# Another order for one quad's second norm and its widening in a fused mixer kernel

## What is computed

```python
x = x + attn_a(layernorm(x))   # state-space mixer: 8 heads, head size 64, state 128, rotated B and C,
                               # h = alpha*h + beta*Bx_prev + gamma*Bx; y = h.C; rmsnorm; out projection
x = x + ffn(layernorm(x))      # r = sigmoid(xr @ W_r); out = r * (relu(xk @ W_k)**2 @ W_v)
x = x + attn_b(layernorm(x))   # in projection to 768 channels, causal filter of 3 taps, product of two thirds,
                               # convolution over 2048 tokens, gate by the last third, out projection
x = x + ffn(layernorm(x))      # the same ffn
```

## Time and profile before

| | us |
|---|---|
| median of the 3 runs | 4767.65 (4763.98 to 4768.28) |
| profiled execution | 4775.44 |
| its span | 4773.7 |

### The profile page before, as it was taken

How to read it: one execution, slowest core, us unless ns; L and a number is a source line. 1 busy time by engine, 2 the same in 40 slices (tenths; PEclk the granted TensorE clock), 3 DMA queues, 4 the chain that set the end, 5 groups by cost and what they waited for, 6 DMA issues and landing times. The chain is left out here.

```text
span 4773.7 us, 118783 instructions
## 1 busy us (share of the span) xinstructions
PE 4307.8 (90%) x39924; PEld 3574.9 (75%) x39924; DVE 3254.1 (68%) x6762; ACT 2160.8 (45%) x5049; POOL 2349.4 (49%) x3277
## 2 busy tenths in 40 slices
PE   5259999999999999999999999999978999989999
PEld 4128777777777777777777777777756888878888
DVE  8456666667676666666676666666644666658888
ACT  3124444444444444444444444444435666645555
POOL 3027666566655666566566656665520000006666
PEclk9669999999999999999999999999988999999999
DMA  8120111111111111111111111111007666643333
GB/s 271 78 79 27 33 47 37 38 41 37 47 37 33 46 37 45 37 35 45 37 41 40 37 45 35 35 47 37 30 29 193 181 185 179 181 124 101 105 104 97
DMA packets 369422, 347.40 MB, mean 73 GB/s; under 512 B 24665, under 2 KB 342937, under 8 KB 359833
## 3 DMA queue, kind: packets, MB, share of 16 engines
q1 hardware_dynamic: 352028, 323.88, 22.8%
q10 hardware_dynamic: 16896, 16.78, 1.0%
HBM read 231.91 MB, written 108.66 MB: 71 GB/s over the span
## 5 line engine op out<-in xcount | busy, mean ns | idle before, releaser
L733 PE MATMUL bank<-w_bc,xnT 128*128 128x512 f32 x3072 | 815.8, 408 | 40.2 <-POOL xnT L1054 40.2
L733 PEld LDWEIGHTS bank<-w_bc,xnT 128*128 128x128 f32 x3072 | 570.2, 192 | 180.3 <-issue 65.6
L936 ACT COPY turned_t<-bank 128x512 f32<-128x512 f32 x512 | 299.6, 585 | 860.8 <-PE bank L756 860.7
L1467 PE MATMUL p_yc<-sig,toep 64*64 64x256 f32 (+14 forms) x16384 | 539.5, 282 | 17.1 <-issue 13.9
L1062 POOL TENSOR_TENSOR steps<-upto,par 128x512 fp32r<-128x512 f32 x512 | 550.4, 1095 | 5.6 <-PE bank L742 5.6
L1467 PEld LDWEIGHTS p_yc<-sig,toep 64*64 64x64 f32 x16384 | 476.9, 132 | 92.7 <-issue 46.3
L1171 DVE TENSOR_TENSOR rot<-bank,par 128x512 f32<-128x512 f32 x512 | 350.6, 685 | 240.8 <-PE bank L733 162.5
L1071 POOL TENSOR_TENSOR turned_b<-rot 128x512 f32<-128x512 f32 x256 | 325.1, 1270 | 308.7 <-DVE rot L1172 308.3
L766 PEld LDWEIGHTS bank<-turned_t 128*128 128x128 f32 x2048 | 301.3, 214 | 127.6 <-issue 104.9
L766 PE MATMUL bank<-turned_t 128*128 128x128 f32 x2048 | 310.5, 301 | 93.5 <-issue 92.0
L1191 DVE TENSOR_TENSOR mix<-bank,decay 128x512 f32<-128x512 f32 x256 | 175.9, 687 | 300.4 <-PE bank L766 299.9
(11 more groups left out here) (259 smaller groups left out, 9741.2 us busy)
## 6 DMA issues: line engine op xcount, KB each, us to landing
toep<-taps_dram SPq DMA_DIRECT2D x256, 260.0 KB, 4.2
el<-el_dram SPq DMA_DIRECT2D x256, 128.0 KB, 3.0
xg<-arg_x SPq DMA_DIRECT2D x32, 512.0 KB, 5.0
xnT_dram<-xt_g ACTq DMA_DIRECT2D x32, 512.0 KB, 5.1
xnT_raw<-xnT_dram SPq DMA_DIRECT2D x128, 128.0 KB, 2.3
x_quad<-arg_x SPq DMA_DIRECT2D x32, 512.0 KB, 3.9
x_dram<-x_quad SPq DMA_DIRECT2D x32, 512.0 KB, 3.7
x0T_dram<-conv SPq DMA_DIRECT2D x32, 512.0 KB, 2.8
```

Source lines behind the costliest of these rows:

```text
L733: last = mm(p_bc[c][:, :], xnT[w.q % 2][p][:, k, :], w_bc[q][:, k, c * 1024 + g * W4:c * 1024 + (g + 1) * W4], start=(n == 0), stop=(n == ...
L936: s_.copy(turned_t[g][c][:, :], p_tr[:, :]).then_inc(s[f"copy_{BC[c]}"], 1)
L1467: last = mm(by_seq(p_y[p][c][odd * H:(odd + 1) * H, 0:2 * TILES])[:, :, first:], toep[n % SLOTS][c * H:(c + 1) * H, lag * H:(lag + 1) * H] ...
```

## The change

It moves steps within the lists of PE, ACT, POOL and DVE. No instruction is added or removed.

- PE: `widen` 5 goes from behind the two first `project_bc` of q=2 to the end of q=1.
- DVE: in q=0, `residual2` 0 goes from ahead of `weigh_gram` 0 to behind `weigh_gram` 1, and `residual2` 1 from there to behind `rotate` (1,0). In q=1, both `x2_lo` go ahead of `cut_decay` 1. In q=2, `taps` 4 goes ahead of `rotate` (0,0) and `taps` 5 ahead of `weigh_gram` 0.
- POOL, q=0: `layer_rstd` 0 goes from behind `fade_state` to behind `add_turned` (1,1), `layer_rstd` 1 from behind `masked_steps` 1 to behind `add_turned` (1,0). `before_filter` stays.
- ACT: in q=0, `normalised` 0 goes behind `exponentials` 0 and `own_bounds` 1, `normalised` 1 behind `copy_turned` (0,0). In q=1 both `x2_hi` go ahead of `square_y`. In q=2 `take_up` 5 goes ahead of `own_bounds` 0.

```diff
--- before.py
+++ after.py
@@ -857,8 +857,6 @@
                 for q in range(QUAD):
                     tile(q, 0, project_bc, 0, 1)
                     tile(q, 0, project_bc, 0, 0)
-                    if q == 2:
-                        quad(2, widen, 5)
                     if q == 3:
                         quad(1, receptance, 0)
                     tile(q, 1, gram, 0)
@@ -901,6 +899,8 @@
                     if q == 2:
                         quad(1, key, 1)
                     tile(q, 0, decay_logs, 1)
+                    if q == 1:
+                        quad(2, widen, 5)
             rounds(body)
 
         @block.scalar
@@ -997,20 +997,18 @@
                 for q in range(QUAD):
                     tile(q, -1, split_xnT)
                     tile(q, 1, exponentials, 1)
-                    tile(q, 2, square_y)
-                    tile(q, 0, own_bounds, 0)
                     if q == 1:
                         quad(2, x2_hi, 0)
                         quad(2, x2_hi, 1)
+                    tile(q, 2, square_y)
                     if q == 2:
                         quad(2, take_up, 5)
+                    tile(q, 0, own_bounds, 0)
                     if q == 3:
                         quad(1, tanh, 0)
                     tile(q, 1, copy_turned, 1, 1)
                     tile(q, 1, copy_turned, 1, 0)
                     tile(q, 2, mean_square, q)
-                    if q == 0:
-                        quad(2, normalised, 2, 0)
                     if q == 1:
                         quad(2, take_up, 0)
                     if q == 2:
@@ -1021,7 +1019,7 @@
                     tile(q, 0, exponentials, 0)
                     tile(q, 0, own_bounds, 1)
                     if q == 0:
-                        quad(2, normalised, 2, 1)
+                        quad(2, normalised, 2, 0)
                     if q == 1:
                         quad(2, take_up, 1)
                         quad(2, take_up, 2)
@@ -1031,6 +1029,8 @@
                     if q == 2:
                         quad(1, relu_squared, 0)
                     tile(q, 0, copy_turned, 0, 0)
+                    if q == 0:
+                        quad(2, normalised, 2, 1)
                     if q == 1:
                         quad(1, normalised, 1, 0)
                         quad(1, normalised, 1, 1)
@@ -1141,14 +1141,15 @@
                     tile(q, 0, add_turned, 0, 0)
                     tile(q, 1, fade_state)
                     if q == 0:
-                        quad(2, layer_rstd, 2, 0)
                         quad(2, before_filter)
                     tile(q, 2, scan_rstd)
                     tile(q, 0, add_turned, 1, 1)
+                    if q == 0:
+                        quad(2, layer_rstd, 2, 0)
                     tile(q, 0, masked_steps, 1)
+                    tile(q, 0, add_turned, 1, 0)
                     if q == 0:
                         quad(2, layer_rstd, 2, 1)
-                    tile(q, 0, add_turned, 1, 0)
                     if q == 1:
                         quad(1, layer_rstd, 1, 1)
                         quad(1, first_column)
@@ -1275,22 +1276,20 @@
             def body(tile, quad, n):
                 for q in range(QUAD):
                     tile(q, 0, rotate, 0, 1)
-                    tile(q, 1, cut_decay, 1)
-                    tile(q, 0, rotate, 0, 0)
-                    if q == 0:
-                        quad(2, residual2, 0)
                     if q == 1:
                         quad(2, x2_lo, 0)
                         quad(2, x2_lo, 1)
+                    tile(q, 1, cut_decay, 1)
                     if q == 2:
                         quad(2, taps, 4)
-                    tile(q, 1, weigh_gram, 0)
+                    tile(q, 0, rotate, 0, 0)
                     if q == 2:
                         quad(2, taps, 5)
+                    tile(q, 1, weigh_gram, 0)
                     tile(q, 0, rotate, 1, 1)
                     tile(q, 1, weigh_gram, 1)
                     if q == 0:
-                        quad(2, residual2, 1)
+                        quad(2, residual2, 0)
                     if q == 1:
                         quad(2, taps, 0)
                     if q == 2:
@@ -1302,6 +1301,8 @@
                     if q == 3:
                         quad(1, gated, 0)
                     tile(q, 0, rotate, 1, 0)
+                    if q == 0:
+                        quad(2, residual2, 1)
                     if q == 1:
                         quad(2, taps, 2)
                     tile(q, 1, carry_state)
```

## The result

Over eight runs the changed kernel takes 4777.51 us (median, 4772.04 to 4783.97), and the kernel before, over eight runs, 4765.81 us (4760.48 to 4777.86). The ratio is 1.0023, with a 95% interval of 1.0012 to 1.0034: 11 us slower, 6 to 16. That is 0.37 us in each of 30 rounds. The forecast was 18 us slower, in a range from 4738 to 4815.

The account below looks back on a forecast made before the run. PE's instruction order, with its waits and low clock, was taken as the bound. Per round -0.75 (q=0), -0.8 (q=1) and +2.15 (q=2) sum to +0.6 us, +18 us over 30 rounds: 4786 us, range 4738 to 4815.

Parts of the forecast that it names:

- q=0: `x2n_over` against the old order at full clock: In q=0, `x2n_over` starts at 1097.7 instead of 1097.02: +0.7 us per round, bounds -0.4 to +1.2.
- q=0: low clock gone: In q=0, the mean clock loss behind the old wait before the second gram goes: -2.15 us per round.
- q=0: low clock behind the new waits: In q=0, two new PE stalls cost clock: 0.7 us per round, bounds 0 and 1.8.
- q=1, at full clock: In q=1, PE's gaps before `sum_over` and `widen` 0 shrink by 0.2 and 0.6 us: -0.8 us per round.
- q=2: `sum_over` later: In q=2, DVE's later chain makes `sum_over` start later: +0.95 us per round, bounds +0.8 to +1.6.
- q=2: more low clock: In q=2, clock loss grows from 0.7 to 1.9 us as PE idles nearly 3 us: +1.2 us per round.
- What goes in q=0: In q=0, PE's second gram starts without its 3.1 us wait, and the clock loss behind it leaves this place.
- What is late next: In q=0, POOL's stream delays the norm: new PE stalls of 0.7 to 1.8 us before `turn_over`, about 2 at `x2n_over`.
- rival B: Whole kernel: one of two clock terms goes the forecast's way, the other not; within 0.3 us per round, 4768; chance 0.20.
- Rival A: q=0: `x2n_over` comes at 1097.0 and its stalls don't lower the clock; -24 us, 4744; chance 0.24.
- C: q=0 and q=2: low clock at both places, and long; +3.4 us per round, 102 us; chance 0.10.
- D: Whole round: POOL and DVE keep ahead everywhere, the stalls really go; 8.3 us per round, 4519 us; chance 0.03.

Follow-up runs that it names:

- e2: Changed kernel with its q=0 part undone (second norm's residual, rstd and normalised steps as before): 4786.95 us, 1.0048 of the kernel before.
- e10: Changed kernel with `before_filter` moved behind `layer_rstd` 1 on POOL in q=0: 4765.1 us, 0.9999 of the kernel before.
- e7: Kernel before with only the q=0 part of the change added: 4737.78 us, 0.9952 of the kernel before.
- e3: Changed kernel with its q=1 part undone (`x2_hi` and `x2_lo` late again): 4789.16 us, 1.0052 of the kernel before.
- e1: Changed kernel with its q=2 part undone (`widen` 5 and its readers back in their old places): 4744.21 us, 0.9962 of the kernel before.
- e4: Changed kernel where a step taking a post bank waits only for the reader of the bank's last use: 4720.67 us, 0.9912 of the kernel before.
- e11: Changed kernel with eight extra constant-weight products on PE before `sum_over` of q=2: 4727.25 us, 0.9921 of the kernel before.
- e5: Changed kernel with `x2n_over` moved behind the first two `project_bc` of q=1: 4705.88 us, 0.9880 of the kernel before.
- e9: Changed kernel with edits of e1, e4, e5, `layer_rstd` 0 ahead of `add_turned` (1,1), q=2's `sum_over` and `xn_over` behind the second gram: 4539.16 us, 0.9533.
- e8: Kernel before with the edit of e4, one wait per use of the two post banks: 4697.00 us, 0.9861 of the kernel before.

## Why the prediction was right, point by point

All in us per round, from the changed kernel's profile, means of 29 rounds.

| step | forecast | measured |
|---|---|---|
| q=0: `x2n_over` against the old order at full clock | +0.7 | +0.7 |
| q=0: low clock gone | -2.15 | -2.15 |
| q=0: low clock behind the new waits | +0.7 | +0.3 |
| q=1, at full clock | -0.8 | -0.2 |
| q=2: `sum_over` later | +0.95 | +0.8 |
| q=2: more low clock | +1.2 | +0.8 |
| sum | +0.6 | +0.3 in the profile (100.69 against 100.46 gives 0.23), 0.37 from the runs |

*What goes in q=0* was right: no wait before L766, and e2 brings 3.1 us of it back. *What is late next* was right in its places and sizes: 1.4 us before L756, 2.2 us before L845. That POOL's stream is the reason was argued in the forecast; e10 shows it, with 1.65 us for 1.54 us of work moved.

*q=1* was mis-sized, -0.2 instead of -0.8 us. The early low parts are worth 0.6 us by themselves (`x2n_over` to `widen` 0 at full clock: 8.81 us in e7 and e3 without them, 8.18 in e1 and 8.20 in the changed kernel with them), since `widen` 0 keeps a wait of 0.25 us. And the forecast left out a loss of 0.4 us (8.44 us before, 8.81 in e7): `x2n_over`, now behind a wait, has 0.34 us of exposed waits inside that the old one, reached with a full queue, did not show. e4 shows what they are.

*q=2* was right in mechanism: the 3.1 us of idle time on DVE stood in the forecast, and so did the later `sum_over`. `sum_over` came 0.8 instead of 0.95 us later, because the cut was not held up by POOL (0.60 us in both kernels, where 0.75 was reckoned).

*The clock terms* were both too high, 0.3 for 0.7 and 0.8 for 1.2. I had taken the first from the nearest stall of the trace, the second from an idle time of nearly 3 us in q=2, where 2.5 us came; the clock fell there in 23 of 29 rounds, against 13 before. e11 confirms that low clock is a cost of its own; e7 and e10 show that its size cannot be read off one stall, since it changes with the timing of the whole round.

The sum is nearer to the forecast than its terms: q=1 gave 0.6 us less than forecast, the clock cost 0.8 us less, and `sum_over` of q=2 0.15 us less. That the first two nearly cancel is luck.

The sum came out at 11 us for 18, just above the 9.5 us that the forecast called measurable, so rival B (no change) is missed narrowly. Rival A fell: `x2n_over` came at its later time and the clock did fall in both places, though less. C did not come: neither stretch of low clock was long, and the idle time of q=2 stayed below 3 us. D fell too. Without its q=2 part the change would have been a gain (e1).

The rule of the Trainium skill (SBUF — State Buffer, "Who interferes with whom"), that VectorE with two SBUF inputs and GpSimd reading SBUF block each other, agrees with the 0.61 and 0.66 us of two tiny POOL operations and the 1.38 us of L1250; how much of the +0.7 us they make up was not measured apart.

## What to carry to other kernels

When a stalled step is moved out of the way, move the whole chain in the reckoning and ask when the fullest engine reaches the next step that waits for it: here one wait of 3.1 us became two of 3.6 us. Moving work ahead of the producer of another engine's head step (`widen` 5 before `project_bc`) delays that engine by the work's full length: DVE's idle time before `rotate` (0,1) went from 1.68 to 3.10 us for 1.40 us of work, and 0.8 us of it reached `sum_over`. And count what TensorE does after a wait, low clock and a list of satisfied waits in the open, beside the wait itself. Putting independent work where the wait was took the wait and its low clock away at `x2n_over` (e5); e9, where it was done at `sum_over` too, along with four other edits, has neither long waits nor more than two spells of low clock in 2800 us.

## What I had not expected of the hardware

- Satisfied waits on PE cost nothing visible while its queue is full, but they do behind a stall: with 14 fewer in front of the second half of `x2n_over` 0.34 us went, and 0.6 us went between the taps and `sum_over` (e4). In the kernel before, removing them gave 1.4%, a part of it clock (e8).
- Added products made the kernel faster, by 1% (e11), since they kept the granted clock at 1.00.
- Moving 1.5 us of POOL work changed the low clock of the stage from 137 to 205 us in 2800, with no wait of PE lengthened (e10). The low spells number 15, 26, 28, 40 and 51 in e7, e1, the changed kernel, the kernel before and e10, whose rounds differ by less than 2 us. What decides in which rounds the clock falls stays open.
